# Two products to a ReLU and scores moved back in the edge stages of a graph network

## The chip, the cores and the metric

The kernel runs as one launch on one core of a Trainium2 chip. The metric is the device time of a launch in microseconds, the median of several runs. Such medians of this kernel can tell a difference of about 0.2% from none.

## What is computed

A graph of 6250 nodes with 256 features and 100000 edges sorted by target (`dst`). Two layers of one kind (4 heads of 64), then one of another (8 heads of 32), with residuals and layer norms around them. The first two layers are, cut down:

```python
xl = (x @ Wl).reshape(n, H, C)
xr = (x @ Wr).reshape(n, H, C)
e = leaky_relu(xl[src] + xr[dst], 0.2)
logits = einsum('ehc,hc->eh', e, att)
m = segment_max(logits, dst, n)
ex = exp(logits - m[dst])
denom = segment_sum(ex, dst, n)
out = segment_sum(xl[src] * (ex / denom[dst])[:, :, None], dst, n)
```

The third layer takes the two parts of its logits from columns of the node products, so it needs no ReLU of 256 columns for each edge.

## The kernel before, in words

Each layer has a node stage (products of all nodes, a table written to memory) and an edge stage. The edge stage cuts the sorted edges into 832 items of 128 edges, each wholly inside one tile of 128 target nodes; 16 items are a group, so there are 52 groups a layer and 156 in all. POOL gathers the table rows of an item's sources into one of 32 slots of `gathered` (L692). PE, ACT and DVE walk through the groups in step; the order on each engine is the order in which its code is written, `body` in `edge_pe`, `edge_act` and `edge_dve`, once per group, with semaphores between them. SyncE loads indices and flags and is not touched.

For item `i` of a group of the first two layers PE does this:

- `expand(i, ...)` (L1069, L1075): for each half of 128 columns three bf16 products and one fp32 transpose add up `z` = `xl[src] + xr[dst]`, turned, in a slot of `pZ`. ACT then writes its ReLU to a slot of `reluT` (L864).
- After each fourth item `scores(k, ...)` (L1083): eight fp32 matmuls that multiply four items' ReLU with the attention weights into `pL`. The trace counts each of them as two.
- `weighed` (L1130): the segment sum of an item that is eight places older, `Dm` by `gathered` into one of four banks of `pS`, which DVE adds to `acc_mem` (L1527). DVE makes `Dm` (L1540) and multiplies the gathered rows by their weights (L1558).

Between these stands the chain of the softmax for the group before, at fixed places of the group: at `i` = 0 the last scores and the linear part close the logits (L1098), ACT copies them to `cT` (L849), DVE scans them for maxima (L1572, L1573); at 2 PE turns the scans' ends (L1113, L1114), ACT copies them out (L873), DVE scans over the items (L1577 to L1586); at 4 PE turns the carry (L1117), DVE forms the maximum and the difference (L1591 to L1595); at 6 PE turns the difference (L1090), ACT takes the exponential; at 8 and 9 the rescaling factor goes through PE (L1120) and ACT (L860). DVE does these steps between its iterations `s`, two items each: the scans after iteration 0, L1577 after iteration 1, L1591 after iteration 2.

What PE waits for around ReLU, and where the scores of four items stand:

```python
if l < 2 and i % Q != 1 and (second or i >= 2):
    pe.wait_ge(relu_done, up(relu_done))
...
if first and l < 2 and i > 0 and i % Q == 0:
    if second and i == Q:
        pe.wait_ge(logits_copied, up(logits_copied))
    scores(i // Q - 1, 1)
```

`z_slot(i)` is one of two banks of `pZ`, so `expand(i)` must wait for the ReLU of item `i - 2`. `Q` is 4. `scores(0)` runs at `i` = 4, after `expand(4)` and before the carry; the scores of items 12 to 15 run at `i` = 0 of the next group.

Of the kernel before, what the change touches and what calls it, by code (L numbers as in the profile page):

```python
# [17 lines left out]
P = 128  # L18
GI = 16
Q = 4  # L20
K4 = GI // Q
ATT0 = K4 - 1
D = 256
# [7 lines left out]
ACT = mybir.ActivationFunctionType  # L31
AX = mybir.AxisListType
F32 = mybir.dt.float32
BF16 = mybir.dt.bfloat16
# [20 lines left out]
def gnn_program(nc, x, src, dst, wl1, wr1, att1, b1, wl2, wr2, att2, b2, w_gat, a_gat, out):  # L55
# [18 lines left out]
    with ExitStack() as ctx:  # L74
# [13 lines left out]
        acc_mem = sb("acc_mem", [P, max(TILES * ROW, scratch_words)])  # L88
        acc = acc_mem[:, 0:TILES * ROW].rearrange("p (t r) -> p t r", r=ROW)
        G = sb("gathered", [P, 2, GI, ROW])  # L90
        rel_items = sb("rel_items", [P, ITEMS])
        last_items = sb("last_items", [P, ITEMS], BF16)
        t_row = sb("t_row", [1, ITEMS], I32)
        ident = sb("ident", [P, P])
# [12 lines left out]
        Dm = sb("Dm", [P, 8, P])  # L107
        src_items = Dm[:].rearrange("p n e -> p (n e)")[:, 0:ITEMS].bitcast(I32)
        s_all = Dm[:].rearrange("p n e -> p (n e)")[:, 0:8 * TILES].rearrange("p (t h) -> p t h", h=8)
        reluT = sb("reluT", [P, 5, D])  # L110
        flags = sb("flags", [P, 2, 4, P])
        F1 = sb("F1", [P, P])
        B1 = sb("B1", [P, P])
# [295 lines left out]
        def in_turns(ap):  # L409

            return ap.rearrange("o h (k a) -> o h k a", a=Q)

        def relu_slot(i):

            return reluT[:, 4 if i % (2 * Q) == Q else i % Q, :]

        def part(t, n):

# [6 lines left out]
        def turned_block(k):  # L425

            return (pL, pM)[k // FB][:, k % FB * BS:(k % FB + 1) * BS]

        def z_slot(i):

            return pZ[:, i % 2, 0:D]


        @block.sync
# [271 lines left out]
        def _(act):  # L706
# [119 lines left out]
            def edge_act(l):  # L826
                H = heads(l)

                def linear(r):

                    if l == 2:
                        nc.scalar.activation(per_h(lin, 8), G[:, r, :, D:ROW], ACT.Copy).then_inc(lin_ready, 1)
                    else:
                        nc.scalar.activation(by_turn(lin[:], 8), G[:, r, :, D:ROW].rearrange("p (k a) h -> p a h k", a=Q), ACT.Copy).then_inc(lin_ready, 1)

                up, settle, state = tally()

                def body(gh, b, first, second, late):
                    c = 1 - b
                    for i in range(GI):  # L840
                        if second and i == 0 and l == 2:
                            before = landed_need(l, gh if b == 1 else gh - 1)
                            before = before if static(before) else act.snap(before)
                            for n in range(GI):
                                act.wait_ge(landed[c][n], before)
                            linear(c)
                        if second and i == 0:
                            act.wait_ge(logits_done, up(logits_done))
                            nc.scalar.activation(cT[:], pL[:, 0:P], ACT.Copy).then_inc(logits_ready, 1)  # L849
                            nc.scalar.activation(first_row[:, 0:1], DT[:, c, 0:1], ACT.Copy).then_inc(logits_copied, 1)  # L850
                        if second and i == 6:
                            act.wait_ge(dif_turned, up(dif_turned))
                            if l == 2:
                                nc.scalar.activation(G[:, c, :, D:ROW], per_h(pM[:, P:2 * P], H), ACT.Exp).then_inc(ex_ready, 1)
                            else:
                                nc.scalar.activation(G[:, c, :, D:D + H].rearrange("p (k a) h -> p a h k", a=Q), by_turn(pM[:, P:2 * P], H),  # L856
                                                     ACT.Exp).then_inc(ex_ready, 1)
                        if second and i == 9:
                            act.wait_ge(fx_spread, up(fx_spread))
                            nc.scalar.activation(resc[:, 0:H], pM[:, 264:264 + H], ACT.Identity, scale=first_row[:, 0:1],  # L860
                                                 bias=first_row[:, 1:2]).then_inc(resc_ready, 1)
                        if first and l < 2:
                            act.wait_ge(zt_done, up(zt_done))
                            nc.scalar.activation(relu_slot(i), z_slot(i), ACT.Relu).then_inc(relu_done, 1)  # L864
                        if second and i == 2:
# [10 lines left out]
                        if second and i == 6:  # L876
                            nc.scalar.activation(me[:], pM[:, 0:P], ACT.Copy).then_inc(m_ready, 1)
                        if second and i == 7:
# [15 lines left out]
        def _(pe):  # L894
# [129 lines left out]
            def edge_pe(l):  # L1024
# [12 lines left out]
                def body(gh, b, first, second, late):  # L1037
# [14 lines left out]
                    def expand(i, freed):  # L1052

                        if i == 0:
                            pe.wait_ge(dt_ready, up(dt_ready))
                        if l < 2 and i % Q != 1 and (second or i >= 2):
                            pe.wait_ge(relu_done, up(relu_done))
                        moving = DT[:, b, i * P:(i + 1) * P]
                        if l == 2:
# [6 lines left out]
                        for q in range(2):  # L1066
# [6 lines left out]
                            if q == 0:  # L1073
                                pe.wait_ge(landed[b][i], here)
                            mm = nc.tensor.matmul(z_slot(i)[:, half], G[:, b, i, half], ident[:], is_transpose=True, start=False, stop=True)  # L1075
                        mm.then_inc(zt_done, 1)

                    def scores(k, more):

                        pe.wait_ge(relu_done, up(relu_done, more))  # L1080
                        for q in range(2):
                            for a in range(Q):
                                nc.tensor.matmul(pL[a * (P // Q):(a + 1) * (P // Q), 0:P], attpad[:, q, ATT0 - k:ATT0 - k + P // Q],  # L1083
                                                 relu_slot(Q * k + a)[:, q * P:(q + 1) * P], start=(k == 0 and q == 0), stop=False)

                    for i in range(GI):
                        freed = (l < 2 or i % 4 == 0) and (late if i <= GI // 2 else second)
                        if second and i == 6:
# [5 lines left out]
                        if second and i == 0:  # L1094
                            if l < 2:
                                scores(K4 - 1, 1 if first else 2)
                            pe.wait_ge(lin_ready, up(lin_ready))
                            nc.tensor.matmul(pL[:, 0:P], lin[:], ident[:], is_transpose=True,  # L1098
                                             start=False, stop=True).then_inc(logits_done, 1)
                        if first and l < 2 and i > 0 and i % Q == 0:  # L1100
                            if second and i == Q:
                                pe.wait_ge(logits_copied, up(logits_copied))
                            scores(i // Q - 1, 1)
                        if second and not first and i == 1:
                            pe.wait_ge(logits_copied, up(logits_copied))
                        if first and l == 2:
                            if second and i == 0:
                                pe.wait_ge(logits_copied, up(logits_copied))
                            expand(i, freed)
                        if second:  # L1110
                            if i == 2:
# [3 lines left out]
                            if i == 4:  # L1115
                                pe.wait_ge(carry_ready, up(carry_ready))
                                nc.tensor.matmul(pM[:, 256:258], carry_in[:], ident[:, 0:33:32], start=True, stop=True).then_inc(carry_turned, 1)  # L1117
                            if i == 8:
# [533 lines left out]
W_STEPS = [6, 12, 27]  # L1652
EARLY = 4
IOTA = 288

# [26 lines left out]
```

## Time and profile before

| what | us |
|---|---|
| median of 3 runs | 4043.88 |
| lowest and highest | 4042.95, 4047.39 |
| profiled execution, first to last instruction | 5270.5 |
| of it, the three edge stages | 4347.6 |
| PE busy | 3942.9 |
| DVE busy | 3296.7 |
| POOL busy | 2645.7 |
| ACT busy | 1199.0 |

For the profiled execution only its span is recorded. Busy shares are averages over stages with different limits. A row's idle time stands before its instructions and is put down to what ended it. Ends of matmuls are modelled, so distances are taken from start to start.

### The profile page before, as it was taken

The page shows a single profiled execution, that of the slowest core. Times are in us where ns is not written, and L with a number is a line of the kernel's source. Part 1 is how long each engine was busy: PE and PEld are TensorE (multiplying, and loading weights), DVE is VectorE, ACT ScalarE, POOL GpSimd, SP SyncE. Part 2 cuts the span into 40 slices and gives each one's busy share as a digit, 9 for nine tenths or more (in the row PEclk, how much of TensorE's full clock was granted, in tenths as well). Part 3 has the DMA queues.
Part 4 walks back from the last instruction along what each step waited for, and adds up shares of the span by engine and source line. Part 5 has one row for each costly group of instructions (what it writes and reads, how often), then busy time and mean ns, then how long its engine had stood idle before and what let it go on. Part 6 is the DMA issues. An engine that isn't in the chain of part 4 may idle for free. (4 is left out here: it accounts for less than half of the span.)

```text
span 5270.5 us, 122213 instructions
## 1 busy us (share of the span) xinstructions
PE 3942.9 (75%) x31349; PEld 2833.8 (54%) x31350; DVE 3296.7 (63%) x9997; ACT 1199.0 (23%) x4200; POOL 2645.7 (50%) x2941
## 2 busy tenths in 40 slices
PE   6588878888878795888887888787566666666666
PEld 5355555565655574555555556555344444444443
DVE  6466666666666762666666666666466666666666
ACT  3322222222222362222222222223100000000002
POOL 4455555555555224555555555543455555555550
PEclk8799999999899997999999999989777777777779
DMA  3333333333333123333333333325444434343333
GB/s 91 97 95 98 96 98 95 97 93 93 96 96 99 50 66 88 98 94 99 95 98 92 100 94 98 94 77 156 118 110 109 110 106 112 108 111 108 108 106 104
DMA packets 333905, 521.10 MB, mean 99 GB/s; under 512 B 152887, under 2 KB 219617, under 8 KB 333809
## 3 DMA queue, kind: packets, MB, share of 16 engines
q0 software_dynamic: 120320, 338.39, 23.8%
q1 hardware_dynamic: 213489, 181.58, 12.1%
q8 instruction: 42, 0.69, 0.1%
q14 instruction: 54, 0.44, 0.0%
HBM read 484.14 MB, written 35.46 MB: 99 GB/s over the span
## 5 line engine op out<-in xcount | busy, mean ns | idle before, releaser
L692 POOL DMA_INDIRECT gathered<-table,idx x2496 | 2452.7, 983 | 2090.4 <-POOLq L358 1516.7
L1130 PE MATMUL pS<-gathered,Dm 128*128 128x264 f32 x4992 | 1860.0, 456 | 193.2 <-issue 63.0
L1527 DVE TENSOR_TENSOR acc_mem<-acc_mem,pS 128x264 f32 x2496 | 1048.2, 420 | 466.8 <-remote 224.2
L1069 PE MATMUL pZ<-DT,x 128*128 128x128 bf16 x9984 | 1206.0, 229 | 167.1 <-ACT reluT L864 99.3
L1069 PEld LDWEIGHTS pZ<-DT,x 128*128 x9984 | 926.6, 102 | 598.2 <-issue 341.3
L864 ACT ACTIVATE reluT<-pZ 128x256 f32<-128x256 f32 x1664 | 610.2, 382 | 1990.8 <-PE pZ L1075 1248.1
L1130 PEld LDWEIGHTS pS<-gathered,Dm 128*128 128x128 f32 x4992 | 876.0, 218 | 324.5 <-issue 146.8
L1075 PE MATMUL pZ<-ident,gathered 128*128 128x128 f32 x3328 | 972.5, 292 | 18.0 <-issue 10.7
L1558 DVE TENSOR_TENSOR gathered<-gathered 128x256 f32<-128x256 f32 x2496 | 945.8, 419 | 60.6 <-ACT gathered L856 28.8
L1083 PE MATMUL pL<-reluT,attpad 128*32 128x128 f32 x6656 | 277.5, 286 | 408.4 <-ACT reluT L864 373.3
L1540 DVE TENSOR_TENSOR Dm<-pS,rel_items 128x256 f32<-128x256 f32 x1239 | 515.0, 416 | 0.0
L1075 PEld LDWEIGHTS pZ<-ident,gathered 128*128 128x128 f32 x3328 | 495.1, 149 | 20.3 <-issue 10.8
L1061 PE MATMUL pL<-DT,x 128*128 128x128 bf16 x2496 | 350.3, 252 | 136.4 <-ACT first_row L850 100.3
L1061 PEld LDWEIGHTS pL<-DT,x 128*128 x2496 | 257.6, 115 | 345.3 <-issue 246.9
L1083 PEld LDWEIGHTS pL<-reluT,attpad 128*32 128x32 f32 x6656 | 163.2, 111 | 473.8 <-ACT reluT L864 267.5
L1572 DVE TENSOR_TENSOR_SCAN F<-flags,cT 128x128 f32<-128x128 f32 x156 | 66.2, 425 | 548.2 <-ACT cT L849 528.3
L622 POOL TENSOR_TENSOR pool_pad<-zeros 128x1 f32<-128x1 f32 x184 | 56.4, 307 | 396.3 <-DVE gathered L1373 189.5
L975 PE MATMUL pS<-W,gathered 128*128 128x260 f32 (+1 forms) x588 | 177.7, 428 | 38.6 <-ACT gathered L762 36.8
L1577 DVE TENSOR_TENSOR_SCAN Fout<-span_row,end_row 1x68 f32<-1x68 f32 (+1 forms) x156 | 52.1, 334 | 242.2 <-ACT end_row L871 142.5
L1117 PE MATMUL pM<-ident,carry_in 128*128 128x2 f32 x312 | 67.9, 287 | 179.0 <-DVE carry_in L1584 151.3
L1591 DVE SCALAR_TENSOR_TENSOR peak<-flags,pM,peak 128x128 f32<-128x128 f32 x156 | 55.4, 355 | 203.4 <-PE pM L1117 180.3
L1117 PEld LDWEIGHTS pM<-ident,carry_in 128*128 128x128 f32 x312 | 55.1, 221 | 208.9 <-DVE carry_in L1584 157.5
(232 smaller groups left out, 3335.0 us busy)
## 6 DMA issues: line engine op xcount, KB each, us to landing
DT<-rel_dram SPq DMA_DIRECT2D x156, 512.0 KB
gathered<-table,idx POOLq DMA_INDIRECT x2496
flags<-flag_dram SPq DMA_DIRECT2D x1664, 8.0 KB
span_row<-flag_dram SPq DMA_DIRECT2D x1664, 0.1 KB
table<-xls SPq DMA_DIRECT2D x147, 132.0 KB
flags<-flag_dram SPq DMA_DIRECT2D x416, 32.0 KB
gathered<-table SPq DMA_DIRECT2D x98, 132.0 KB, 2.1
gathered<-in_x SPq DMA_DIRECT2D x98, 128.0 KB, 2.1
```

Of the source, the lines that this page charges most:

```text
L692: nc.gpsimd.indirect_dma_start(out=G[:, b, i, :], out_offset=None, in_=tab[l], in_offset=bass.IndirectOffsetOnAxis(ap=idx[:, b, i:i + 1], ...
L864: nc.scalar.activation(relu_slot(i), z_slot(i), ACT.Relu).then_inc(relu_done, 1)
L975: mm = nc.tensor.matmul(pX[:, b, 0:width], hT[:, b, q * P:(q + 1) * P], W[:, q, 0:width], start=(q == 0), stop=(q == 1))
L1061: mm = nc.tensor.matmul(pL[:, 0:P], s3[:, bass.ds(tk[i], 1), s, GI - 1 - i:9 * GI - 1 - i].rearrange("p o c -> p (o c)"), moving, start=(i ...
L1069: mm = nc.tensor.matmul(z_slot(i)[:, half], x3[:, bass.ds(tk[i], 1), s, half].rearrange("p o c -> p (o c)"), moving, start=(s == 0), stop= ...
L1075: mm = nc.tensor.matmul(z_slot(i)[:, half], G[:, b, i, half], ident[:], is_transpose=True, start=False, stop=True)
L1083: nc.tensor.matmul(pL[a * (P // Q):(a + 1) * (P // Q), 0:P], attpad[:, q, ATT0 - k:ATT0 - k + P // Q], relu_slot(Q * k + a)[:, q * P:(q + ...
L1117: nc.tensor.matmul(pM[:, 256:258], carry_in[:], ident[:, 0:33:32], start=True, stop=True).then_inc(carry_turned, 1)
L1130: nc.tensor.matmul(pS[:, i % 4, 0:ROW], Dm[:, i % 8, :], G[:, at[0], at[1], :], start=True, stop=True).then_inc(seg_done, 1)
L1527: link(v.tensor_tensor(acc_at(n), acc_at(n), pS[:, n % 4, 0:ROW], ALU.add))
L1540: ins = v.tensor_tensor(Dm[:, 2 * p % 8:2 * p % 8 + 2, :], numbers.unsqueeze(1).to_broadcast([P, 2, P]), rel.unsqueeze(2).to_broadcast([P, ...
L1558: ins = v.tensor_tensor(gv, gv, row[:, D:D + H].unsqueeze(2).to_broadcast([P, H, D // H]), ALU.mult)
```

## The change

In the first two layers two items share a bank of `pZ`, and one ReLU of 512 columns serves both: PE signals `zt_done` after the odd item only, ACT works at odd `i`, and the two banks now hold four items. `expand(i)` waits for ReLU at even `i` alone. `reluT` grows from five item slots to three pairs; `rel_items` becomes bf16 (whole numbers below 128) and so takes half the room. `scores(k)` for the first three quads runs at `i` = 4k + 6 rather than 4k + 4, with no wait for ReLU of its own; the last quad's stays at `i` = 0 of the next group. `after(l)` is 0 with `LOGITS = 0`, so the chain's steps keep their places in all three layers.

```diff
-        rel_items = sb("rel_items", [P, ITEMS])
+        rel_items = sb("rel_items", [P, ITEMS], BF16)
-        reluT = sb("reluT", [P, 5, D])
+        reluT = sb("reluT", [P, 3 * 2, D])
+        def relu_pair(i):
+
+            pair = 1 if i % Q > 1 else i // Q % 2 * 2
+            return reluT[:, 2 * pair:2 * pair + 2, :].rearrange("p i c -> p (i c)")
+
         def relu_slot(i):
-
-            return reluT[:, 4 if i % (2 * Q) == Q else i % Q, :]
+            return relu_pair(i)[:, i % 2 * D:(i % 2 + 1) * D]
+        def z_pair(i):
+
+            return pZ[:, i // 2 % 2, 0:2 * D]
+
         def z_slot(i):
-
-            return pZ[:, i % 2, 0:D]
+            return z_pair(i)[:, i % 2 * D:(i % 2 + 1) * D]
+
+        def after(l):
+
+            return LOGITS if l < 2 else 0
...
-                        if first and l < 2:
+                        if first and l < 2 and i % 2:
                             act.wait_ge(zt_done, up(zt_done))
-                            nc.scalar.activation(relu_slot(i), z_slot(i), ACT.Relu).then_inc(relu_done, 1)
+                            nc.scalar.activation(relu_pair(i), z_pair(i), ACT.Relu).then_inc(relu_done, 1)
...
-                        if l < 2 and i % Q != 1 and (second or i >= 2):
+                        if l < 2 and i % 2 == 0 and (i >= Q or second and i < LOGITS + 1):
                             pe.wait_ge(relu_done, up(relu_done))
...
-                        mm.then_inc(zt_done, 1)
+                        if i % 2:
+                            mm.then_inc(zt_done, 1)
...
-                        pe.wait_ge(relu_done, up(relu_done, more))
+                        if more:
+                            pe.wait_ge(relu_done, up(relu_done, more))
...
-                        if first and l < 2 and i > 0 and i % Q == 0:
-                            if second and i == Q:
+                        if first and l < 2 and i > Q and i % Q == 2:
+                            if second and i == Q + 2:
                                 pe.wait_ge(logits_copied, up(logits_copied))
-                            scores(i // Q - 1, 1)
+                            scores(i // Q - 1, 0)
...
+LOGITS = 0
```

PE at item 4 of a group in the loop, before: the last transpose of `expand(4)`, the scores of the first quad, the carry, the segment sum of an older item, and the start of `expand(5)`.

```order
L1075 MATMUL pZ<-ident,gathered 128x128
L1083 MATMUL pL<-reluT,attpad 32x128 [waits relu_done,logits_copied]
L1083 MATMUL pL<-reluT,attpad 32x128 x7
L1117 MATMUL pM<-ident,carry_in 128x2 [waits carry_ready]
L1130 MATMUL pS<-gathered,Dm 128x264 [waits added]
L1069 ISA
L1069 MATMUL pZ<-DT,x 128x128
```

PE at the same place of the change (line numbers 11 to 13 higher):

```order
L1086 MATMUL pZ<-ident,gathered 128x128
L1130 MATMUL pM<-ident,carry_in 128x2 [waits carry_ready]
L1143 MATMUL pS<-gathered,Dm 128x264 [waits added]
L1080 ISA
L1080 MATMUL pZ<-DT,x 128x128
```

The scores are gone from between `expand(4)` and the carry.

PE at item 6, before: the end of item 5, the wait for the difference, the start of `expand(6)`.

```order
L1075 MATMUL pZ<-ident,gathered 128x128
L1130 MATMUL pS<-gathered,Dm 128x264 [waits wg_done]
L1090 MATMUL pM<-ident,dif 128x128 [waits dif_ready]
L1091 MATMUL pM<-ident,mT 128x128
L1069 ISA [waits relu_done]
```

PE at item 6 of the change, the same place:

```order
L1086 MATMUL pZ<-ident,gathered 128x128
L1143 MATMUL pS<-gathered,Dm 128x264 [waits wg_done]
L1103 MATMUL pM<-ident,dif 128x128 [waits dif_ready]
L1104 MATMUL pM<-ident,mT 128x128
L1080 ISA [waits relu_done]
```

PE a little later in the change, at the end of `expand(6)`:

```order
L1086 MATMUL pZ<-ident,gathered 128x128
L1096 MATMUL pL<-reluT,attpad 32x128 [waits logits_copied]
L1096 MATMUL pL<-reluT,attpad 32x128 x7
L1143 MATMUL pS<-gathered,Dm 128x264 [waits added]
L1080 ISA
```

The eight score matmuls now stand behind the wait for `dif_ready` and behind `expand(6)`.

ACT in a group, before, from the copy of the logits to that of the maxima (`me`):

```order
L849 ACTIVATE cT<-pL 128x128 [waits logits_done]
L850 ACTIVATE first_row<-DT 128x1
L864 ACTIVATE reluT<-pZ 128x256 [waits zt_done] x3
L873 ACTIVATE end_row<-pM 1x4x16 [waits ends_turned]
L873 ACTIVATE end_row<-pM 1x4x16
L875 ACTIVATE first_row<-DT 128x1
L864 ACTIVATE reluT<-pZ 128x256 [waits zt_done] x3
L856 ACTIVATE gathered<-pM 128x4x4x4 [waits dif_turned]
L864 ACTIVATE reluT<-pZ 128x256 [waits zt_done]
L877 ACTIVATE me<-pM 128x128
L864 ACTIVATE reluT<-pZ 128x256 [waits zt_done]
```

ACT in the change, the same stretch and the next steps:

```order
L860 ACTIVATE cT<-pL 128x128 [waits logits_done]
L861 ACTIVATE first_row<-DT 128x1
L875 ACTIVATE reluT<-pZ 128x512 [waits zt_done]
L884 ACTIVATE end_row<-pM 1x4x16 [waits ends_turned]
L884 ACTIVATE end_row<-pM 1x4x16
L886 ACTIVATE first_row<-DT 128x1
L875 ACTIVATE reluT<-pZ 128x512 [waits zt_done] x2
L867 ACTIVATE gathered<-pM 128x4x4x4 [waits dif_turned]
L888 ACTIVATE me<-pM 128x128
L875 ACTIVATE reluT<-pZ 128x512 [waits zt_done]
L891 ACTIVATE fr<-fr 1x4 [waits drop_ready]
```

Three single ReLUs became one or two of double width, and `me` no longer has a ReLU in front of it.

## Rows read from the trace of the kernel before

**Rows 1.** The page's head.

```profile
span 5270.5 us, 122213 instructions
```

**Rows 2.** Windows, three edge stages together: busy time (instructions) by engine, clock, DMA.

```profile
sum 4347.60, PE 3330.36 PEld 2388.05 DVE 2785.82 ACT 873.52 POOL 2359.73; mean PE 1110.12 PEld 796.02 DVE 928.61 ACT 291.18 POOL 786.58
```

**Rows 3.** Groups by line, PE, first two edge stages: busy, mean | idle before, releasers.

```profile
L1083 PE MATMUL pL<-reluT,attpad 128*32 128x128 f32 x6596 | 274.8, 285 | 388.1 <-ACT reluT L864 353.1 <-issue 35.0
...
L1090 PE MATMUL pM<-ident,dif 128*128 128x128 f32 x103 | 36.7, 356 | 38.2 <-DVE dif L1595 35.5 <-issue 2.6
```

**Rows 4.** Timeline of PE, one group of stage one: start, length, line, count [idle].

```profile
1014.54 0.65 PE L1083 MATMUL pL<-reluT,attpad 128*32 128x128 f32 x16
1015.12 0.33 PE L1098 MATMUL pL<-ident,lin 128*128 128x128 f32 x1
1015.28 0.61 PE L1130 MATMUL pS<-gathered,Dm 128*128 128x264 f32 x2
...
1017.31 0.27 PE L1113 MATMUL pM<-ident,F 128*1 128x128 f32 x1
1017.42 0.27 PE L1114 MATMUL pM<-ident,B 128*1 128x128 f32 x1
1017.53 0.61 PE L1130 MATMUL pS<-gathered,Dm 128*128 128x264 f32 x2
1017.97 0.33 PE L1069 MATMUL pZ<-DT,x 128*128 128x128 bf16 x3
...
1018.54 0.61 PE L1130 MATMUL pS<-gathered,Dm 128*128 128x264 f32 x2
...
1024.58 0.33 PE L1090 MATMUL pM<-ident,dif 128*128 128x128 f32 x1 [1.42 <-DVE dif L1595]
```

**Rows 5.** Timeline of DVE, the same group.

```profile
1015.91 0.42 DVE L1572 TENSOR_TENSOR_SCAN F<-flags,cT 128x128 f32<-128x128 f32 x1 [3.18 <-ACT cT L849]
...
1016.57 0.40 DVE L1527 TENSOR_TENSOR acc_mem<-acc_mem,pS 128x264 f32 x1
...
1019.55 0.29 DVE L1577 TENSOR_TENSOR_SCAN Fout<-span_row,end_row 1x68 f32<-1x68 f32 x1 [1.24 <-ACT end_row L873]
...
1020.61 0.43 DVE L1527 TENSOR_TENSOR acc_mem<-acc_mem,pS 128x264 f32 x1
...
1021.63 0.76 DVE L1558 TENSOR_TENSOR gathered<-gathered 128x256 f32<-128x256 f32 x2
1023.45 0.36 DVE L1591 SCALAR_TENSOR_TENSOR peak<-flags,pM,peak 128x128 f32<-128x128 f32 x1 [1.07 <-remote]
...
1024.24 0.29 DVE L1595 TENSOR_TENSOR dif<-cT,mT 128x128 f32<-128x128 f32 x1
```

**Rows 6.** Timeline of all engines, first full group of stage two.

```profile
2051.16 0.27 PE L1113 MATMUL pM<-ident,F 128*1 128x128 f32 x1
...
2051.97 0.29 DVE L1577 TENSOR_TENSOR_SCAN Fout<-span_row,end_row 1x68 f32<-1x68 f32 x1 [1.34 <-ACT end_row L873]
...
2053.82 0.38 PE L1117 MATMUL pM<-ident,carry_in 128*128 128x2 f32 x2
...
2054.06 0.33 PE L1069 MATMUL pZ<-DT,x 128*128 128x128 bf16 x3
...
2054.24 0.36 DVE L1591 SCALAR_TENSOR_TENSOR peak<-flags,pM,peak 128x128 f32<-128x128 f32 x1 [1.25 <-PE pM L1117]
```

**Rows 7.** Timeline of POOL, one gather in stage one.

```profile
1022.60 0.95 POOL L692 DMA_INDIRECT gathered<-table,idx  x1 [0.30 <-issue]
```

**Rows 8.** Groups by line and shape, ACT, whole run: busy, mean ns.

```profile
L864 ACT ACTIVATE reluT<-pZ 128x256 f32<-128x256 f32 x1664 | 610.2, 382 | 1990.8 <-PE pZ L1075 1248.1 <-remote 530.3 <-issue 211.4
...
L849 ACT ACTIVATE cT<-pL 128x128 f32<-128x128 f32 x156 | 43.2, 277 | 407.5 <-remote 214.4 <-PE pL L1098 133.7 <-issue 59.4
```

**Rows 9.** Groups by line and shape, DVE, whole run: busy, mean ns.

```profile
L1540 DVE TENSOR_TENSOR Dm<-pS,rel_items 128x256 f32<-128x256 f32 x1239 | 515.0, 416 | 0.0
...
L1434 DVE TENSOR_TENSOR gathered<-gathered,x 128x256 f32<-128x256 f32 x6 | 2.5, 423 | 0.1
```

More of the change, by code:

```diff
@@ L846, in body @@
                             linear(c)
-                        if second and i == 0:
+                        if second and i == 2 * after(l):
                             act.wait_ge(logits_done, up(logits_done))
@@ L850, in body @@
                             nc.scalar.activation(first_row[:, 0:1], DT[:, c, 0:1], ACT.Copy).then_inc(logits_copied, 1)
-                        if second and i == 6:
+                        if second and i == 6 + after(l):
                             act.wait_ge(dif_turned, up(dif_turned))
@@ L857, in body @@
                                                      ACT.Exp).then_inc(ex_ready, 1)
-                        if second and i == 9:
+                        if second and i == 9 + after(l):
                             act.wait_ge(fx_spread, up(fx_spread))
@@ L861, in body @@
                                                  bias=first_row[:, 1:2]).then_inc(resc_ready, 1)
-                        if first and l < 2:
+                        if first and l < 2 and i % 2:
                             act.wait_ge(zt_done, up(zt_done))
-                            nc.scalar.activation(relu_slot(i), z_slot(i), ACT.Relu).then_inc(relu_done, 1)
-                        if second and i == 2:
+                            nc.scalar.activation(relu_pair(i), z_pair(i), ACT.Relu).then_inc(relu_done, 1)
+                        if second and i == 2 + after(l):
                             act.wait_ge(ends_turned, up(ends_turned))
@@ L875, in body @@
                             nc.scalar.activation(first_row[:, 1:2], DT[:, c, 0:1], ACT.Copy, scale=-1.0, bias=1.0).then_inc(dt_free, 1)
-                        if second and i == 6:
+                        if second and i == 6 + after(l):
                             nc.scalar.activation(me[:], pM[:, 0:P], ACT.Copy).then_inc(m_ready, 1)
-                        if second and i == 7:
+                        if second and i == 7 + after(l):
                             act.wait_ge(drop_ready, up(drop_ready))
@@ L1087, in body @@
                         freed = (l < 2 or i % 4 == 0) and (late if i <= GI // 2 else second)
-                        if second and i == 6:
+                        if second and i == 6 + after(l):
                             pe.wait_ge(dif_ready, up(dif_ready))
@@ L1093, in body @@
                             expand(i, freed)
-                        if second and i == 0:
+                        if second and i == after(l):
                             if l < 2:
@@ L1099, in body @@
                                              start=False, stop=True).then_inc(logits_done, 1)
-                        if first and l < 2 and i > 0 and i % Q == 0:
-                            if second and i == Q:
+                        if first and l < 2 and i > Q and i % Q == 2:
+                            if second and i == Q + 2:
                                 pe.wait_ge(logits_copied, up(logits_copied))
-                            scores(i // Q - 1, 1)
-                        if second and not first and i == 1:
+                            scores(i // Q - 1, 0)
+                        if second and not first and i == after(l) + 1:
                             pe.wait_ge(logits_copied, up(logits_copied))
@@ L1110, in body @@
                         if second:
-                            if i == 2:
+                            if i == 2 + after(l):
                                 pe.wait_ge(scan_done, up(scan_done))
@@ L1114, in body @@
                                 nc.tensor.transpose(pM[0:1, P:2 * P], B1[:, 0:1], ident[:]).then_inc(ends_turned, 1)
-                            if i == 4:
+                            if i == 4 + after(l):
                                 pe.wait_ge(carry_ready, up(carry_ready))
                                 nc.tensor.matmul(pM[:, 256:258], carry_in[:], ident[:, 0:33:32], start=True, stop=True).then_inc(carry_turned, 1)
-                            if i == 8:
+                            if i == 8 + after(l):
                                 pe.wait_ge(fx_ready, up(fx_ready))
```

## The prediction

> **What bounds the kernel now.** I read the page's head first, then busy time by stage, the groups of waits, and last the timelines of one group on PE and DVE. The profiled execution spans 5270.5 us [rows 1], of which the three edge stages take 4347.6 [rows 2]; 922.9 lie around them. The median is 4043.9, so the profile stretches the program by 30%, and the question is where. If all the stretch lies in the edge stages, a group of the timed runs takes (4043.9 - 922.9) / 156 = 20.0 us against 27.9 in the profile; if the rest shrinks by a tenth too, 20.6. These are estimates, but the rows bear them out. In steady stretches PE takes 0.44 us for a segment sum and 0.57 for an `expand` (1017.53 to 1017.97 to 1018.54), 0.58 for a quad of scores (1014.54 to 1015.12), 0.16 for the linear part, 0.22 for the two turns of the scans [rows 4], and 0.24 for the carry (2053.82 to 2054.06) [rows 6]. A group of the first two stages is 16 x 1.01 + 4 x 0.58 + 0.62, and some 0.46 for two steps like the last two: 19.6 us of PE. POOL needs 0.30 + 0.95 us for a gather [rows 7], 20.0 for 16. So the timed runs go at about the pace of PE and of the gathers, with at most some 1 us of waiting in a group.
>
> The profile shows much more. PE sat idle 388 us before the scores, nearly all put down to ReLU [rows 3], in 416 quads: 0.93 us each. The cause lies further back. After the carry at 1020.93 DVE went on only at 1023.45, 2.52 us later, and not for lack of its own work (1.07 idle, released by something the profile does not name) [rows 4, 5]; in the first full group of stage two the same step took 0.42 (2053.82 to 2054.24) [rows 6]. What PE signals arrives up to 2 us late in some stretches of the profiled execution. A ReLU that starts so late makes the scores wait. With groups of 20.0 us there is no room for 3.7 us of it in each, so I take the sum from the steady rows.
>
> **The change part by part.** *ReLU.* A ReLU of 256 columns takes 382 ns, a copy of 128 columns 277 [rows 8]: 0.82 ns a column, so 512 columns should take about 592 (estimate). ACT is saved 16 x 382 - 8 x 592 = 1.4 us a group, and nobody waits for ACT's busy time, so I count 0. Before, ReLU of item 4k + 3 has the segment sum and the next `expand`, 1.01 us, before the scores ask for it, which covers 0.38; after, the first three quads have two more items. For the last quad the double ReLU comes 0.21 later against the same 1.01: covered too. Behind this ReLU on ACT waits the linear part, which PE needs 0.58 later, after the scores. Without this cover it would be 0.21 x 104 = 22 us slower. At the other places where ACT waits for an odd item's product (behind it stand the exponentials and the rescaling factor), PE has gone past that item already. `me` gets out earlier by a ReLU, for nobody late.
>
> *rel_items in bf16.* The trace has one operation of this size with one fp32 and one bf16 input: 423 ns, against 416 for `Dm` today [rows 9]. Between 0 and 7 ns x 8 x 104 = 6 us on DVE; I take 0.
>
> *Scores of three quads, two items later.* PE's work in the group is the same, 19.6 us. But the first quad's 0.58 us leaves the stretch between the closed logits (L1098) and the wait for `dif_ready` (L1090). Counted from L1098, PE reaches that wait after 0.16 + 6 x 0.44 + 5 x 0.57 + 0.22 + 0.58 + 0.24 = 6.69 us today, and after 6.11 in the change. DVE's path from L1098 [rows 4, 5]: scans start at 0.79 (1015.12 to 1015.91) and take 0.66; an iteration (two adds, `Dm`, two multiplies) 1.78 (1020.61 to the end of 1021.63 + 0.76); L1577 to the next add 1.06; a second iteration 1.78; L1591 to the end of `dif` 1.08; PE sees it 0.05 later. Sum: 7.20. Nothing else is late there: L1577 could start at 0.16 + 2 x 0.44 + 2 x 0.57 + 0.81 (2051.16 to 2051.97 [rows 6]) = 2.99 and DVE comes at 3.23; the carry is ready at 4.29, PE comes at 4.42 without the scores, and its answer 0.42 later finds DVE busy until 6.07. So DVE paces this stretch: PE waits 0.51 today and 1.09 after, and the scores that once filled the time are still to be done. Behind the waiting L1090 stand on PE `expand(6)`, the scores and all later segment sums; DVE, two microseconds ahead by the end of the group, cannot give it back. SyncE's and POOL's queues get no step moved; slots come free with `expand`, late by the same amount.
>
> The added wait costs 0.58 x 104 = 60 us if the rows hold in the timed runs, and 0 if DVE's path is there below 6.11. The rows lie a good 0.5 on the costly side, but they come from a stretched execution; I take three quarters, 0.44 x 104 = 46 us. Sum: 4043.9 + 46 = 4090. In the profiled execution the late signals come on top, and the scores' waits will mostly go, so its span may well shrink while the median grows.
>
> [...] PE gives half as many `zt_done` signals, 832 fewer. Rows first: two equal turns, L1113 without a signal and L1114 with one, each take 0.11 to the next start [rows 4], so a signal costs PE at most 0.01 us, 0 here. [...]
>
> **The rivals.** *Not slower: the scores wait for ReLU in the timed runs as well.* For it: the largest PE wait of the profile [rows 3], and a margin of half a microsecond that one late signal uses up. Against it: the 20.0 us. At most about 0.6 us a group can be such waiting (the 20.6 above), so it gives back up to 62 us: 3982, or some 4005 where part of the loss at `dif_ready` is paid as well. It decides once the waits before scores, per group, exceed what `dif_ready` adds.
>
> *No difference.* DVE's path is under 6.1 us without the profiler, or the gathers' 20.0 us pace covers what PE loses; 4036 to 4052. Against it: 20.65 is above 20.0, and the path would have to be a sixth shorter than its rows.
>
> *All of it and more.* The full 60 us, and the last quad's ReLU uncovered, 22: 4126.
>
> [...]
>
> **How the numbers follow.** My forecast has 0.47, the increments 0.03, all of it and more 0.07, no difference 0.14, not slower by waits that go 0.29. Three runs tell about 0.2%, 8 us, from none. Slower by more: 0.47 + 0.03 + 0.07 = 0.57; within: 0.14; faster: 0.29. The forecast's own range is 4055 to 4112. The range of 4000 to 4118 leaves out most of the last rival above 4118, and the deeper half of the faster one, together no more than 0.2.
>
> **What would show it.** In the changed profile: idle time before L1090's line above 0.7 us a group where it is 0.37 now (38.2 in 103 [rows 3]), with `dif` as releaser, and before the scores less than 100 us in place of 388; DVE's idle time before the scans about as now; 832 ReLUs of about 0.59 us. If idle time before L1090 stays at 0.37 or falls, the added wait is wrong; if the median falls below 4036, the scores' wait was real in the timed runs, and the step "no room for it" failed.

## The result, and the profile after

| | median, us | lowest to highest | runs |
|---|---|---|---|
| before | 4045.04 | 4038.15 to 4053.91 | 11 |
| after | 4053.75 | 4049.50 to 4058.21 | 11 |

The ratio is 1.0021, 95% interval 1.0013 to 1.0030: slower by 8.7 us, just past what can be told from no change, where the forecast was 46 us slower. The sign was right; the time lies below the forecast's own range.

The profiled execution of the changed kernel is not stretched as that of before was [rows 1]: its span is the time of the timed runs. For a fair comparison the kernel before was therefore profiled again (first experiment), and that execution was not stretched either. The page of the changed kernel, its head and groups (busy, mean ns | idle before, releaser):

```profile
span 4050.6 us, 121279 instructions
PE 3584.3 (88%) x31349; PEld 2640.1 (65%) x31350; DVE 3234.9 (80%) x9997; ACT 1121.1 (28%) x3368; POOL 2686.6 (66%) x2941
L875 ACT ACTIVATE reluT<-pZ 128x512 f32<-128x512 f32 x832 | 496.7, 597 | 1263.8 <-PE pZ L1086 1210.2
L1096 PE MATMUL pL<-reluT,attpad 128*32 128x128 f32 x6656 | 268.9, 279 | 0.5 <-ACT reluT L875 0.5
```

Its first edge stage as a window (51 groups: us, busy time of PE, PEld, DVE, ACT and POOL, clock, DMA share, GB/s), then the gathers on POOL in that stage:

```profile
216.60:1306.60 1090.00, 1069.57 (x11863) 833.54 (x11859) 903.84 (x2896) 341.65 (x918) 811.86 (x811) 1.00 0.48 131
```

```profile
L703 POOL DMA_INDIRECT gathered<-table,idx x798 | 798.0, 1000 | 265.8 <-issue 142.7 <-POOLq L358 114.5 <-PE pZ L1080 8.7
```

The 832 double ReLUs take 597 ns (592 was the estimate from [rows 8]), and the scores wait for ReLU 0.5 us in the whole run, where [rows 3] had 388. The wait for `dif` in the first stage, by group of instructions on PE, changed kernel:

```profile
L1103 PE MATMUL pM<-ident,dif 128*128 128x128 f32 x50 | 16.4, 328 | 13.3 <-DVE dif L1608 13.3
```

That is 0.27 us of recorded idle time in every one of the 50 groups. One group on PE shows where it stands (timeline; start, length, line, count [idle before]); it answers to [rows 4]:

```profile
793.00 0.65 PE L1096 MATMUL pL<-reluT,attpad 128*32 128x128 f32 x16
793.57 0.33 PE L1111 MATMUL pL<-ident,lin 128*128 128x128 f32 x1
...
798.19 0.28 PE L1130 MATMUL pM<-ident,carry_in 128*128 128x2 f32 x2
798.58 0.71 PE L1143 MATMUL pS<-gathered,Dm 128*128 128x264 f32 x2
...
799.70 0.61 PE L1143 MATMUL pS<-gathered,Dm 128*128 128x264 f32 x2
800.57 0.33 PE L1103 MATMUL pM<-ident,dif 128*128 128x128 f32 x1 [0.27 <-DVE dif L1608]
...
801.57 0.64 PE L1096 MATMUL pL<-reluT,attpad 128*32 128x128 f32 x16
802.14 0.71 PE L1143 MATMUL pS<-gathered,Dm 128*128 128x264 f32 x2
```

The same stretch on DVE, which answers to [rows 5]:

```profile
794.25 0.42 DVE L1585 TENSOR_TENSOR_SCAN F<-flags,cT 128x128 f32<-128x128 f32 x1 [3.22 <-ACT cT L860]
...
798.11 0.42 DVE L1553 TENSOR_TENSOR Dm<-pS,rel_items 128x256 f32<-128x256 f32 x1
798.44 0.42 DVE L1540 TENSOR_TENSOR acc_mem<-acc_mem,pS 128x264 f32 x1
798.78 0.75 DVE L1571 TENSOR_TENSOR gathered<-gathered 128x256 f32<-128x256 f32 x2
799.45 0.35 DVE L1604 SCALAR_TENSOR_TENSOR peak<-flags,pM,peak 128x128 f32<-128x128 f32 x1
...
800.23 0.29 DVE L1608 TENSOR_TENSOR dif<-cT,mT 128x128 f32<-128x128 f32 x1
```

From L1111 (793.57) to the turn of `dif` (800.57) it is 7.00 us; DVE works without a gap from its first scan, as the working had it (7.20). PE waits twice. The turn of `dif` comes 0.87 us after the start of the segment sum before it (799.70), where 0.44 is that sum's own [rows 4]: 0.43 us are lost, of which the modelled end of the matmul leaves 0.27 to be counted as idle. Another 0.15 is lost where the segment sum at 798.58, 0.39 behind the carry that takes 0.24 [rows 6], follows the end of `Dm` (798.11 + 0.42). Together that is 0.58; over the stage the two distances are 0.42 and 0.13 longer than with the scores in their old places (second experiment). The scores come at 801.57, behind the wait. The mechanism of the forecast is there in each group. What hid its price?

### The profile page after: what moved, and what is told of

It reads as the page before. It is cut to its first block and busy times, and to the rows that moved or that the text cites. A ratio compares the mean times of both kernels' runs of the same rounds, so it can differ in the third digit from the quotient of the medians.

```text
span 4050.6 us, 121279 instructions
## 1 busy us (share of the span) xinstructions
PE 3584.3 (88%) x31349; PEld 2640.1 (65%) x31350; DVE 3234.9 (80%) x9997; ACT 1121.1 (28%) x3368; POOL 2686.6 (66%) x2941
## 5 line engine op out<-in xcount | busy, mean ns | idle before, releaser
L703 POOL DMA_INDIRECT gathered<-table,idx x2496 | 2492.0, 998 | 842.5 <-issue 525.0
L1143 PE MATMUL pS<-gathered,Dm 128*128 128x264 f32 x4992 | 1714.3, 427 | 116.9 <-DVE Dm L1553 54.8
L1080 PE MATMUL pZ<-DT,x 128*128 128x128 bf16 x9984 | 1068.2, 220 | 11.7 <-POOL x L661 7.1
L1080 PEld LDWEIGHTS pZ<-DT,x 128*128 x9984 | 865.7, 99 | 302.5 <-issue 30.8
L1143 PEld LDWEIGHTS pS<-gathered,Dm 128*128 128x128 f32 x4992 | 792.9, 199 | 297.8 <-DVE Dm L1553 113.7
L1086 PE MATMUL pZ<-ident,gathered 128*128 128x128 f32 x3328 | 934.7, 281 | 15.9 <-DMA gathered<-table,idx 15.9
L875 ACT ACTIVATE reluT<-pZ 128x512 f32<-128x512 f32 x832 | 496.7, 597 | 1263.8 <-PE pZ L1086 1210.2
L986 PEld LDWEIGHTS pS<-W,gathered 128*128 128x128 f32 x588 | 105.9, 200 | 73.2 <-ACT gathered L773 52.6
L1500 DVE TENSOR_SCALAR DT<-DT,iota_part 128x2048 bf16<-128x2048 bf16 x156 | 116.4, 746 | 27.2 <-DMA DT<-rel_dram 27.1
L1111 PE MATMUL pL<-ident,lin 128*128 128x128 f32 x156 | 53.0, 339 | 83.9 <-ACT lin L843 83.7
```

What stands on the lines that cost most here:

```text
L703: nc.gpsimd.indirect_dma_start(out=G[:, b, i, :], out_offset=None, in_=tab[l], in_offset=bass.IndirectOffsetOnAxis(ap=idx[:, b, i:i + 1], ...
L875: nc.scalar.activation(relu_pair(i), z_pair(i), ACT.Relu).then_inc(relu_done, 1)
L986: mm = nc.tensor.matmul(pX[:, b, 0:width], hT[:, b, q * P:(q + 1) * P], W[:, q, 0:width], start=(q == 0), stop=(q == 1))
L1080: mm = nc.tensor.matmul(z_slot(i)[:, half], x3[:, bass.ds(tk[i], 1), s, half].rearrange("p o c -> p (o c)"), moving, start=(s == 0), stop= ...
L1143: nc.tensor.matmul(pS[:, i % 4, 0:ROW], Dm[:, i % 8, :], G[:, at[0], at[1], :], start=True, stop=True).then_inc(seg_done, 1)
L1500: v.tensor_scalar(DT[:, b, :], DT[:, b, :], iota_part[:, 0:1], None, ALU.is_equal).then_inc(dt_ready, 1)
```

## The experiments

Each is timed over five rounds, but for the first. The time of before differed from job to job, that is, between sets of runs made together (4043.63, 4021.67, 4046.93 us), so differences are taken inside a job where there is a choice.

**The kernel before, profiled again** (no edit).

> The kernel before once more, for a profile that is not stretched (the one of the changed kernel spans 4050.6 us, near its median). Theory A, the prediction's: PE reaches L1090 within 0.1 us of dif and waits at most 0.3 us a group there; PE waits before the scores are near 0; the group of stage one takes about 21.3 us. Theory B, the rival that scores wait for ReLU in timed runs too: idle time before the scores of 0.3 to 0.6 us a group, and a small one at L1090. In the changed kernel a group takes 21.38 us with 0.27 us idle at that place; since it is only 9 us slower, either the wait was there before as well (theory C: nothing was added), or something gave about 0.5 us a group back.

One run, 4053.62 us, above the timed runs of its own job (4039.03 to 4048.03) and within those of the result; span 4051.8. Windows over 51 groups of each of the first two edge stages (columns as above), kernel before, then POOL and PE by group in the first stage:

```profile
216.80:1303.30 1086.50, 1071.13 (x11863) 836.34 (x11859) 911.71 (x2896) 403.34 (x1326) 833.89 (x811) 1.00 0.48 132
1567.60:2657.90 1090.30, 1073.36 (x11864) 837.01 (x11860) 912.34 (x2896) 403.34 (x1326) 838.34 (x811) 1.00 0.48 131
```

```profile
L692 POOL DMA_INDIRECT gathered<-table,idx x798 | 819.8, 1027 | 243.2 <-issue 161.9 <-POOLq L358 78.6 <-PE pZ L1069 2.8
```

```profile
L1069 PE MATMUL pZ<-DT,x 128*128 128x128 bf16 x4788 | 520.9, 220 | 3.4 <-ACT reluT L864 2.6 <-issue 0.5
L1075 PE MATMUL pZ<-ident,gathered 128*128 128x128 f32 x1597 | 448.8, 281 | 10.7 <-DMA gathered<-table,idx 10.7
L1083 PE MATMUL pL<-reluT,attpad 128*32 128x128 f32 x3200 | 128.9, 279 | 0.0
L1090 PE MATMUL pM<-ident,dif 128*128 128x128 f32 x50 | 14.5, 291 | 0.0
```

A group takes 1086.5 / 51 = 21.3 us, not the 20.0 of the forecast. POOL's idle time is 243.2 / 798 = 0.305 us before each gather, the 0.30 of [rows 7], and no single one is above 0.32; so POOL never waited for a slot, and 16 x (819.8 + 243.2) / 798 = 21.3: the gathers alone make the group's time. PE waits for landings (10.7 us), hardly for ReLU (2.6 in `expand`, 0.0 before the scores), and not for `dif` (0.0). In the changed kernel POOL's idle time is 265.8 / 798 = 0.333 us: 37 gaps are longer than 0.32, up to 2.3 us, so there POOL did wait for slots.

**The pairs kept, the scores back** (first of the two parts alone).

```diff
-                        if l < 2 and i % 2 == 0 and (i >= Q or second and i < LOGITS + 1):
+                        if l < 2 and (i % Q == 0 and i >= Q or second and i < LOGITS + 1):
...
-                        if first and l < 2 and i > Q and i % Q == 2:
-                            if second and i == Q + 2:
+                        if first and l < 2 and i > 0 and i % Q == 0:
+                            if second and i == Q:
...
-                            scores(i // Q - 1, 0)
+                            scores(i // Q - 1, 1)
```

> The changed kernel with the scores of each quad back at item 4k + 4, where they wait for the pair's ReLU; pairs, banks and bf16 stay. Theory A (the move of the scores costs about 0.57 us a group at the wait for dif, and pairing gives back): about 3995 us, idle time at dif near 0. Theory B (what gave time back is that scores no longer wait for ReLU): as slow as before or slower, 4045 to 4065, with idle time before the scores, since the double ReLU ends 0.2 us later than a single one. Theory C (neither does anything): 4045 to 4054.

3989.27 us (3986.08 to 3990.99), ratio to before 0.9865 [0.985, 0.988]: faster than both kernels. Window of its first stage (51 groups: 20.7 us each), and POOL there:

```profile
214.90:1271.60 1056.70, 1053.36 (x11864) 832.59 (x11861) 905.59 (x2896) 341.61 (x918) 800.92 (x812) 1.00 0.49 136
```

```profile
L703 POOL DMA_INDIRECT gathered<-table,idx x797 | 785.5, 986 | 245.5 <-issue 150.3 <-POOLq L358 87.3 <-PE pZ L1080 7.9
```

PE is busy for all but 3 us of 1057, and a gather takes 986 ns where it took 1027. Pairing alone, counted at 0 in the forecast, is worth 54 us. Moving the scores on top of it costs 64 (4053.75 - 3989.27). Here the gathers, 16 x (785.5 + 245.5) / 797 = 20.7 us, and PE's own work are level.

**The move alone** (kernel before with the scores at the new places; seven ReLU slots so that single ReLUs are not overwritten, and `rel_items` in bf16 to make room for them).

```diff
-        reluT = sb("reluT", [P, 5, D])
+        reluT = sb("reluT", [P, 7, D])
...
-                        if first and l < 2 and i > 0 and i % Q == 0:
-                            if second and i == Q:
+                        if first and l < 2 and i > Q and i % Q == 2:
+                            if second and i == Q + 2:
...
-                            scores(i // Q - 1, 1)
+                            scores(i // Q - 1, 0)
```

> The kernel before with the scores alone moved to item 4k + 6: single ReLUs in seven slots, two banks of one item each, bf16 rel_items to make room. Theory A: about 4045 + 50, 4085 to 4105. Theory B: near the changed kernel, 4045 to 4060, no idle time before scores and some at dif. Theory C: 4045 within 8.

4053.18 us (4049.51 to 4055.07), ratio 1.0023 [1.0014, 1.0032]: no different from the whole change, so pairing that was worth 54 us alone is worth nothing beside the move. Groups on PE in its first stage:

```profile
L1091 PE MATMUL pM<-ident,dif 128*128 128x128 f32 x50 | 16.4, 328 | 13.3 <-DVE dif L1596 13.3
```

The same 0.27 us. Costs that do not add up mean that two things limit a group in turn: theory G, the gathers in the kernel before; theory A, the wait for `dif` in the changed one. Theory M keeps one limit, PE and DVE's chain, and puts pairing's gain down to `me`, which comes a ReLU earlier.

**`me` ahead of the ReLU** (kernel before).

```diff
+                        if second and i == 6:
+                            nc.scalar.activation(me[:], pM[:, 0:P], ACT.Copy).then_inc(m_ready, 1)
                         if first and l < 2:
...
-                        if second and i == 6:
-                            nc.scalar.activation(me[:], pM[:, 0:P], ACT.Copy).then_inc(m_ready, 1)
```

> The kernel before, with one edit: in item 6's step ACT copies `me` (128x128) ahead of the ReLU of that item, where it stood behind it. Theory G (the kernel before goes at the pace of the gathers on POOL, and pairing the ReLUs made the gathers shorter by moving DVE's work against them): `me` is earlier by a ReLU, about 0.3 us, DVE's wait for it (0.35 us a group in the unstretched profile) goes, and the time changes only as far as DVE's work falls otherwise on the gathers: 4030 to 4050. Theory M (what pairing gave back is `me` alone, on the path that sets the end): 0.35 x 104 = 36 us less, about 4008, and the two turns of POOL and PE move with it.

3999.42 us against 4021.67, ratio 0.9947 [0.9934, 0.9961]. Both numbers missed: 22 us is more than G expected and less than M. By itself it does not tell them apart; its gathers take 992 ns (the kernel before was not profiled in this job).

**The rescaling ahead of the two products** (kernel before).

```diff
+                        if second and s == 5 and l < 2:
+                            dve.wait_ge(resc_ready, up(resc_ready))
...
+                            v.tensor_tensor(ah, ah, resc[:, 0:H].unsqueeze(2).to_broadcast([P, H, D // H]), ALU.mult)
...
-                        if second and s == 5:
+                        if second and s == 5 and l == 2:
```

> The kernel before, with one edit in the first two stages: DVE rescales the accumulator (two multiplies with `resc`) ahead of the two multiplies of `gathered` in iteration 5, where it did so behind them. Same work, another moment. Theory G: the gather that now takes 1.6 to 1.8 us in 28 of 44 groups, always the same slot of the group and always beside these DVE operations, meets other operations; if its length falls to the usual 1.0 us, 0.4 to 0.7 us a group go, 4000 to 4020; if the collision is only moved to another gather, 4044. In either case the long gathers stand at another slot. Theory M: nothing on the path moves earlier, `resc` is waited for a little sooner: 4044 to 4060, long gathers where they were.

4002.99 us against 4021.67, ratio 0.9959 [0.9945, 0.9972]. G expected 4000 to 4020 and M 4044 or more. By the edit nothing that PE waits for comes earlier; the gathers of its first stage:

```profile
L692 POOL DMA_INDIRECT gathered<-table,idx x797 | 796.9, 1000 | 242.9 <-issue 190.5 <-POOLq L358 52.1 <-PE pZ L1069 0.3
```

Still 0.305 us between two gathers, so POOL still paces. That a gather takes 27 ns less than in the first experiment is not all due to the edit, since that profile is of another job, with a slower kernel before; the 18.7 us timed are 11 ns for each of the 1664 gathers of two stages.

**A weak relief** (64 rows in a group's last gather; half of item 15's rows left out), in both kernels.

```diff
+                        rows = P // 2 if short and i == GI - 1 else P
...
-                            out=G[:, b, i, :], out_offset=None, in_=tab[l],
+                            out=G[0:rows, b, i, :], out_offset=None, in_=tab[l],
```

> The kernel before, but in the first two edge stages, from the third group on, the last of a group's 16 gathers takes 64 rows in place of 128 (half the rows of item 15 are left out; all else is computed as before). Theory G: gathers pace this kernel, so a group gets shorter by what the gather loses, some 0.3 to 0.5 us, until PE's and DVE's chain takes over: 4044 - 104 x 0.4 = about 4002, no lower than 3985. Theory M (PE's and DVE's chain paces it, the gathers follow): no change, 4040 to 4048, and POOL waits where it did not.

> The changed kernel with the same relief (64 rows in the last gather of a group of the first two stages, the other half of item 15 left out). Theory A (the changed kernel is paced by PE's wait for `dif`, which the scores' move made 0.57 us longer, and its gathers wait for PE to free slots): no change, 4049 to 4056. Theory G for both kernels (the gathers pace the changed kernel as well): about 4012, as much less as the kernel before loses by the relief.

Before 4013.36 (ratio 0.9979 [0.997, 0.9988]), changed kernel 4052.63. The first is inconclusive: the gather of 64 rows took 0.91 us at its shortest against 0.94 for one of 128, and 1.01 and 1.04 in the mean for its two buffers, so there was little to win. The second fits A, and tells something more: where before ran at 4021.67, this one ran at the same 4052 as ever. The changed kernel does not follow the gathers.

**A strong relief** (15 gathers in place of 16), in both kernels.

```diff
+                        if short and i == GI - 1:
+                            continue
...
-                                pe.wait_ge(landed[b][i], here)
+                                if i < GI - 1:
+                                    pe.wait_ge(landed[b][i], here)
```

> The kernel before, but in the first two edge stages, from the third group on, a group gathers 15 items in place of 16 (item 15 keeps the rows of the first groups; this part of the computation is left out). The relief of 64 rows was too weak to tell: that gather took 0.91 us against 0.95. Theory G (the gathers pace the kernel before at 21.0 to 21.4 us a group, PE alone would need 20.6): POOL needs 15 x 1.34 = 20.0 us a group, PE takes over, some 3985 to 3995, and POOL waits for free slots. Theory M (the chain of PE and DVE paces it): 4020 to 4045, as the kernel before.

> The changed kernel with the same relief: 15 gathers a group in the first two stages, the same part left out. Theory A (PE waits for `dif` with the first quad's scores still to do; this paces the changed kernel at 21.4 us): 4048 to 4056, unchanged. Theory G for both kernels (the gathers pace the changed kernel as well): 3985 to 4000, as the kernel before with the same relief.

Before 3992.66 (3991.10 to 3994.00), 54 us less than 4046.93; changed kernel 4050.58. This decides it. POOL by group, the kernel before with the relief, then the changed one:

```profile
L694 POOL DMA_INDIRECT gathered<-table,idx x748 | 754.8, 1009 | 282.5 <-POOLq L358 140.2 <-issue 135.3 <-PE pZ L1075 7.0
```

```profile
L705 POOL DMA_INDIRECT gathered<-table,idx x747 | 739.5, 990 | 323.6 <-POOLq L358 153.1 <-issue 148.4 <-PE pZ L1086 22.0
```

POOL now waits, 0.38 and 0.43 us before a gather in place of 0.305. With the gathers out of the way the change costs 4050.58 - 3992.66 = 57.9 us. And the kernel before, without pairs, reaches the time of the pairs (3989.27, in another job): pairing's gain was in the gathers, and M falls. The relief did not work through DVE, whose busy time in the stage stays at 911 us. From start to start, the items of a group take as long as in the first experiment within 0.02 us, but for 6, 7, 15 and the part of 0 up to the linear part, which are 0.29, 0.06, 0.10 and 0.09 us shorter (means of the first stage): that half microsecond is what PE had lost to the gathers.

**Only the first quad late** and **only the first quad back** (changed kernel; where the moved scores wait for ReLU again, `expand` does so no longer).

```diff
-                        if first and l < 2 and i > Q and i % Q == 2:
+                        if first and l < 2 and i in (Q + 2, 2 * Q, 3 * Q):
```

```diff
-                        if first and l < 2 and i > Q and i % Q == 2:
+                        if first and l < 2 and i in (Q, 2 * Q + 2, 3 * Q + 2):
```

> The changed kernel with the scores of the second and third quad back at their old places (items 8 and 12, waiting for their ReLU); only the first quad's stand two items later (item 6, behind the wait for `dif`). Against the run with all three back (3989 us) it differs in the first quad alone. Theory A (the whole loss is that the first quad's 0.58 us leave the stretch that DVE paces): 4048 to 4056, idle time of some 0.27 us a group before the turn of `dif`. Rival L (each moved quad costs a third, by order on PE or by slots): about 4010.

> The changed kernel with only the first quad's scores back at item 4, waiting for their ReLU; the second and third quad's stand two items later as in the change. Theory A: the loss goes, 3985 to 3995, and no idle time before the turn of `dif`. Rival L: two thirds of the loss stay, about 4032.

4037.40 and 3995.48 us. PE's wait for `dif` in their first stage, one after the other:

```profile
L1103 PE MATMUL pM<-ident,dif 128*128 128x128 f32 x50 | 16.4, 328 | 13.3 <-DVE dif L1608 13.3
```

```profile
L1103 PE MATMUL pM<-ident,dif 128*128 128x128 f32 x51 | 14.3, 281 | 0.3 <-DVE dif L1608 0.3
```

Bringing back the first quad gives 55 us (from 4050.58, the changed kernel with 15 gathers in the same job) and takes the wait away. Leaving only that quad late keeps the wait, yet the time is 11 us below what A allowed: the other two quads' places are worth 13 us (4050.58 - 4037.40) that A did not have. Rival L's thirds fall by both. Most of the 13 us stands at two places: from start to start (means of the first stage) item 4 takes 1.64 us in the changed kernel against 1.59 with only the first quad late, the part of item 0 up to L1111 1.38 against 1.29, of 0.16 us that a group is longer. At item 4 it is the wait for `Dm` (the segment sum starts 0.38 us behind the carry against 0.34); why item 0 is longer is not shown.

A shift of the whole chain by two items beside the scores was not tried: as written, PE would have read `gathered` for a segment sum while DVE could still be writing it.

## Why the prediction was right in sign and wrong in size

*The stretched profile.* Right: the 388 us of score waits were the stretched profile's alone. The rival built on them (not slower, 3982 to 4005) falls: unstretched, PE waited 0.0 us before the scores in the first stage of the kernel before, and 2.6 us for ReLU in `expand`. That the span would shrink while the median grew came true by luck: the kernel before, unchanged, has a span of 4051.8 without the stretch.

*The added wait.* Right in mechanism, and the difference is right in size: PE loses 0.55 us more a group at `Dm` and `dif` together (0.13 + 0.42, means of the stage) where 0.58 was counted, and the full price of 0.58 x 104 = 60 us stands beside 57.9 measured once the gathers do not limit. That is partly luck. The working put PE half a microsecond too early at `dif` in both kernels: a wait of 0.51 before and 1.09 after, where the runs have none before and 0.55 after. DVE's path is 7.00 us in the group shown, not 7.20, and PE's is longer than was counted, since a quad of scores was priced at 0.58 us, from its start to the next instruction. In the changed kernel an item with a quad takes 1.78 us and one without 1.01, so it is 0.77: beside it `expand` takes 0.65 rather than 0.57 and the segment sum 0.55 rather than 0.44. The timeline of PE shows both (starts of `expand` in three items, with the quad in the first):

```profile
784.73 0.33 PE L1080 MATMUL pZ<-DT,x 128*128 128x128 bf16 x3
...
785.38 0.64 PE L1096 MATMUL pL<-reluT,attpad 128*32 128x128 f32 x16
785.96 0.71 PE L1143 MATMUL pS<-gathered,Dm 128*128 128x264 f32 x2
786.51 0.33 PE L1080 MATMUL pZ<-DT,x 128*128 128x128 bf16 x3
...
787.52 0.33 PE L1080 MATMUL pZ<-DT,x 128*128 128x128 bf16 x3
```

So PE before came to `dif` not 0.51 us early but just in time (idle 0.0), and PE's own work in a group is 20.65 us (1053.36 / 51 with the scores back), not 19.6. Nor is all of the 57.9 the first quad's, as the working had it: with that quad alone late the time is 13 us less (4037.40 against 4050.58), and the two other quads were counted at nothing. The forecast's own sign (0.37 us a group or less before `dif`, and the added wait is wrong) would have rejected it at 0.27: it was read off the stretched profile, while the unstretched kernel before has 0.0.

*The step that failed* is the pace: "POOL needs 0.30 + 0.95 us for a gather, 20.0 for 16. So the timed runs go at about the pace of PE and of the gathers", and with it the reason against the rival of no difference, "20.65 is above 20.0". The 0.95 us was the term that was too small: one row of a gather stood for all. Over the first stage of the kernel before a gather takes 1.03 us, 16 make 21.3, and this was the limit before: above PE's 20.65, and as much as the changed kernel's own 21.4 (1090.0 / 51). The loss at `dif` fell into time that PE spent waiting for gathers anyway:

| | 16 gathers | 15 gathers |
|---|---|---|
| before | 4046.93 | 3992.66 |
| changed | 4053.75 | 4050.58 |
| change | +7 (+8.7 in its own job) | +58 |

The rival "the gathers' pace covers what PE loses" was the right one, with its bounds at 4036 to 4052, just under what was measured; the factor of three quarters on the wait was a guess at the wrong place. How much is covered hangs on the gathers of the job: where the kernel before ran at 4021.67, the changed one, with the weak relief that left it as it was, took 4052.63, 31 us more. So the 8.7 us is no fixed price of this change.

*ReLU pairing at 0.* Beside the move that is what it came to (4053.18 without, 4053.75 with). Alone it was worth 54 us, which no step had, since it does not act through ACT's waiters but on the length of POOL's gathers (986 ns against 1027 in the first stage).

*The increments.* The chances hold 0.03 for time saved by 832 fewer signals; no run shows the cost of a signal that this needs. From start to start, in the changed kernel, an item that signals (13) and one that does not (12) both take 1.01 us, as do items 9 to 11 in the kernel before, where each one signals (means of the first stage). The rows of the forecast hold, 0.01 us a signal at most, and that rival falls.

*The last quad's ReLU and rel_items* cost nothing that shows: 0.5 us idle before the scores in the whole run, and the pairs with the scores back, which have both, run at 3989.27, no slower than the 3992.66 of the kernel before without its gathers' limit.

## What to carry to other kernels

Before a change on one engine is priced, find the resource that never waits. Here it was POOL, whose gaps were all the same smallest one (0.305 us in the mean, none above 0.32); its gathers made the 21.3 us of a group, and one in 16 left out took 54 us off. The mean of a step over a stage (1.03 us), not a clean row (0.95), is its price. A cost that lands beside such a limit is hidden until the limit is lifted (here 7 us against 58), and a gain beside another limit is hidden too (pairing, 54 us alone and none beside the move): run the two parts of a change apart, and both again with the suspected limit relieved. Work that an engine does while another finishes a chain is free only there (the first quad's place, 55 us of time); look which piece fills that gap before moving it.

## What the runs showed of the hardware

A gather on POOL has no fixed length: 0.94 to 1.80 us in the first stage of the kernel before, from 235 us on. Timelines of POOL and of DVE, kernel before, unstretched:

```profile
780.87 1.06 POOL L692 DMA_INDIRECT gathered<-table,idx  x1 [0.30 <-POOLq L358]
782.23 1.80 POOL L692 DMA_INDIRECT gathered<-table,idx  x1 [0.30 <-POOLq L358]
784.34 0.95 POOL L692 DMA_INDIRECT gathered<-table,idx  x1 [0.31 <-POOLq L358]
```

```profile
782.04 0.74 DVE L1558 TENSOR_TENSOR gathered<-gathered 128x256 f32<-128x256 f32 x2
782.72 0.41 DVE L1615 TENSOR_TENSOR acc_mem<-acc_mem,resc 128x256 f32 x1
783.05 0.14 DVE L1616 TENSOR_TENSOR acc_mem<-acc_mem,resc 128x4 f32 x1
```

The gather of 1.80 us lies beside four DVE operations in a row (L1558 twice, L1615, L1616); its neighbours take 0.95 and 1.06. In 34 of that stage's 50 groups a gather began 0.48 us before the rescaling (L1615), as this one did, and 28 of them took 1.73 to 1.80 us. With DVE's order changed (the rescaling first) no gather of the first stage was above 1.25 us from 235 us on. Overlap alone is not the cause: the other 6 of the 34 took 1.04 us, and in the run with the scores back the 16 gathers that began 0.4 us before the rescaling took 0.94 to 0.96. What else decides was not settled.

The time of before is also less fixed than that of the changed kernel: 4021.67 to 4046.93 between the three jobs of the experiments, which ran on three chips, while the changed kernel and its two reliefs stayed between 4050.58 and 4053.75. Whether the chip or the job makes the difference was not tried.
